# Counting edges per node and relation in a graph network: superblocks of layer 0 with every four groups in place of six, and a group's counts added two groups later

## The reference

```python
def _rgcn_layer(x, src, dst, edge_type, w_rel, root, bias):
    seg = dst * NUM_REL + edge_type                 # NUM_REL = 10
    sums = segment_sum(x[src], seg, N * NUM_REL)
    cnt = segment_sum(ones(seg.shape), seg, N * NUM_REL)
    mean = (sums / maximum(cnt, 1.0)[:, None]).reshape(N, NUM_REL, -1)
    return einsum('nrd,rdo->no', mean, w_rel) + x @ root + bias
edge_type = argmax(msg[:, 16:26], axis=1)
h = relu(_layernorm(x))
h = relu(_rgcn_layer(h, src, dst, edge_type, w_rel1, root1, b1))
x = x + _rgcn_layer(h, src, dst, edge_type, w_rel2, root2, b2)
```

## The kernel before

| u | TensorE | ScalarE |
| --- | --- | --- |
| 0 | | square root |
| 1 | transposes | norm and relu |
| 2 | root, chunks 0 to 3 | copy of the transposes |
| 3 | chunks 4 to 7 | copy of root, copies 0 to 3 |
| 4 | chunks 8 to 11 | copies 4 to 7 |
| 5 | | copies 8 to 11 |

## Time and profile before

### The profile page before, as it was taken

How to read it: one execution, slowest core, us unless ns; L and a number is a source line. 1 busy time by engine, 2 the same in 40 slices (tenths; PEclk the granted TensorE clock), 3 DMA queues, 4 the chain that set the end, 5 groups by cost and what they waited for, 6 DMA issues and landing times.

```text
span 17665.0 us, 179568 instructions
## 1 busy us (share of the span) xinstructions
PE 7873.9 (45%) x36107; PEld 6273.0 (36%) x36108; DVE 6843.6 (39%) x28057; ACT 3221.2 (18%) x6961; POOL 10730.4 (61%) x10236
## 2 busy tenths in 40 slices
PE   5633333623333333333333333333333577777777
PEld 3333333322222223332332322222222455555555
DVE  8522222244444423323322222344544344444443
ACT  3422222300000000000000000000000144444443
POOL 0266666365555546666566666666666268888882
PEclk8755555856666555555555555555555577777775
DMA  2333333411111131111111111233333266666665
GB/s 102 125 88 89 89 88 88 175 47 53 54 54 53 53 104 53 52 52 51 51 46 46 47 47 47 60 87 85 87 86 87 66 113 118 117 117 118 117 118 122
DMA packets 1122539, 1438.17 MB, mean 81 GB/s; under 512 B 211981, under 2 KB 737444, under 8 KB 1122316
## 3 DMA queue, kind: packets, MB, share of 16 engines
q0 software_dynamic: 536912, 792.85, 21.0%
q1 hardware_dynamic: 531700, 613.30, 11.9%
q10 hardware_dynamic: 53748, 30.36, 0.6%
HBM read 1101.27 MB, written 334.40 MB: 81 GB/s over the span
## 4 chain that ended last, share of the span: by engine, by line
another core or an unknown queue 29%; issue 22%; DVE 21%; DMA 10%; POOL 6%; PE 5%; ACT 3%; DVEq 2%; ACTq 1%; SPq 0%; POOLq 0%
DMA agg_dram<-acc,sum_row 9%; DVE tab_s L1950 5%; POOL agg_dram L887 5%; DVE scratch L1950 4%; DVE xn_h L1958 3%; DVE scratch L1920 3%; DVE acc L1906 2%; DVE rows L1818 1%; PE ps L1604 1%; POOL scratch L901 1%; ACT hT_s L1009 1%; PE ps L1361 1%; PE ps L1561 1%; PE ps L1562 1%
## 5 line engine op out<-in xcount | busy, mean ns | idle before, releaser
L901 POOL DMA_INDIRECT scratch<-table_dram,row_st x4160 | 3966.4, 953 | 2541.5 <-ACT row_st L1040 1269.3
L901 POOL DMA_INDIRECT rows<-table_dram,row_st x4160 | 3964.0, 953 | 2321.5 <-issue 1247.3
L1361 PE MATMUL ps<-tab_s,rows 128*128 128x128 f32 x8320 | 1906.8, 390 | 3028.0 <-issue 1274.0
L1361 PE MATMUL ps<-scratch 128*128 128x128 f32 x8320 | 1829.5, 390 | 2873.1 <-DMA scratch<-table_dram,row_st 1247.8
L887 POOL DMA_INDIRECT agg_dram<-acc,sum_row x1664 | 2654.5, 1595 | 529.2 <-issue 391.2
L1361 PEld LDWEIGHTS ps<-tab_s,rows 128*128 128x128 f32 x8320 | 1694.4, 294 | 3214.8 <-issue 2149.0
L1361 PEld LDWEIGHTS ps<-scratch 128*128 128x128 f32 x8320 | 1617.8, 289 | 3058.3 <-issue 2119.2
L1906 DVE TENSOR_TENSOR acc<-ps,acc 128x128 f32 x2080 | 608.6, 293 | 4575.8 <-remote 4054.7
L1950 DVE TENSOR_SCALAR scratch<-ps,rw_st 128x128 f32<-128x128 f32 x3328 | 1114.3, 401 | 338.4 <-issue 227.4
L1920 DVE SCALAR_TENSOR_TENSOR scratch<-iota,rw_st,ps 128x128 f32<-128x128 f32 x2496 | 715.2, 343 | 1355.3 <-remote 873.9
L1950 DVE TENSOR_SCALAR tab_s<-ps,rw_st 128x128 f32<-128x128 f32 x3328 | 1112.2, 401 | 330.3 <-issue 247.0
(11 more groups left out here) (229 smaller groups left out, 10600.9 us busy)
## 6 DMA issues: line engine op xcount, KB each, us to landing
scratch<-in_src_row SPq DMA_DIRECT2D x832, 256.0 KB
table_dram<-tab_s POOLq DMA_DIRECT2D x200, 640.0 KB, 3.2
scratch<-type_dram SPq DMA_DIRECT2D x416, 256.0 KB
scratch<-in_dst_row SPq DMA_DIRECT2D x416, 256.0 KB
rows<-table_dram,row_st POOLq DMA_INDIRECT x4160
scratch<-table_dram,row_st POOLq DMA_INDIRECT x4160
scratch<-table_dram SPq DMA_DIRECT2D x416, 64.0 KB
agg_dram<-acc,sum_row POOLq DMA_INDIRECT x1664
```

Of the source, the lines that this page charges most:

```text
L901: pool.indirect_dma_start(row_banks[bank][:, u, :], None, table_dram[k], bass.IndirectOffsetOnAxis(ap=row_st[:, bank, u:u + 1], axis=0)).t ...
L1361: mm = pe.matmul(ps[bank][:, q * P:(q + 1) * P], rows[:, u, :], hot[:, u, :], start=u % QUAD == 0, stop=u % QUAD == QUAD - 1)
```

## The change

`SPAN` goes from 6 to 4, so all 25 superblocks are woven into the first 100 groups, `left` is 0, and `early_rest` and `early_whole` do nothing. `STAGES`, the number of buffers for staged destinations, goes from 3 to 4. Root, chunks and copies are put into `u` 2 and 3: six chunks each, on both engines. The additions of group g-2 now stand inside VectorE's part of group g, one behind each four one-hots; the wait for the products of group g-2 stands ahead of the group. `flow_keep` and `flow_init` each get a wait for their own instruction.

```diff
-SPAN = 6
-STAGES = 3
+SPAN = 4
+STAGES = 4
...
                 elif u == 2:
                     early_hT(f)
+                    early_root(f, at)
+                    early_chunks(f, range(e_chunks // 2))
                 else:
-                    if u == 3:
-                        early_root(f, at)
-                    early_chunks(f, range((u - 3) * e_chunks // 3, (u - 2) * e_chunks // 3))
+                    early_chunks(f, range(e_chunks // 2, e_chunks))
...
                 if u == 2:
                     early_root(f)
-                if 2 <= u < 5:
-                    early_products(f, range((u - 2) * e_chunks // 3, (u - 1) * e_chunks // 3))
+                    early_products(f, range(e_chunks // 2))
+                if u == 3:
+                    early_products(f, range(e_chunks // 2, e_chunks))
...
                 dve.tensor_scalar(acc_f, acc_f, keep, bias_once, ALU.mult, ALU.add).then_inc(s_keep, 1)
+                dve.wait_ge(s_keep, so_far(reps, k, has_src, t) + 2)
...
+                dve.wait_ge(s_init, so_far(reps, k, has_root, t) + 2)
...
-            def count_group(r, g, u):
+            def count_group(r, g, u, before=None):

                 turn = dve.snap(r * ngroups + g)
                 bank = u % 2
+                if before is not None:
+                    t, win = dve.snap(turn - 2), windows(dve, before)
+                    dve.wait_ge(n_mm, t + 2)
                 dve.wait_ge(n_staged, turn + 1)
...
                     i.then_inc(n_hot, 1)
+                    if before is not None:
+                        window = counts[:, bass.ds(win[q], P)]
+                        dve.wait_ge(n_add, t * 4 + (q + 8))
+                        dve.tensor_tensor(window, ps[7 * bank][0:NCNT, q * P:(q + 1) * P], window, ALU.add).then_inc(n_add, 1)
...
                         for u in range(1, SPAN):
-                            count_group(r, u, u)
-                            count_adds(dve.snap(t0 + (u - 1)), u - 1, (u - 1) % 2)
+                            count_group(r, u, u, u - 2 if u > 1 else None)
```

More of the change, by code:

```diff
@@ L1864, in count_pass @@
                                 for u in range(SPAN):
-                                    count_group(r, dve.snap(first + u), u)
-                                    count_adds(dve.snap(t0 + first + (u - 1)), dve.snap(first + (u - 1)), (u + 1) % 2)
+                                    count_group(r, dve.snap(first + u), u, dve.snap(first + u - 2))
                                     if u == 0:
@@ L1870, in count_pass @@
                         g = SPAN * mixed + u
[L1871 to L1874, removed]
+                        count_group(r, g, u, g - 2 if g > 1 else None)
+                    for g in range(max(ngroups - 2, 0), ngroups):
+                        count_adds(dve.snap(t0 + g), g, g % 2)
                     dve.wait_ge(n_add, r * (4 * ngroups) + (4 * ngroups + 8))
```

## The result

| us | before | after |
| --- | --- | --- |
| median (14 runs of each, taken in turn) | 17678.61 | 17724.08 |
| lowest and highest | 17663.2, 17702.44 | 17695.3, 17800.06 |
| span of the profiled execution | 17665.0 | 17722.3 |
| counts stored (counting's end) | 627.57 | 758.51 |
| ScalarE begins the first pass | 772.77 | 806.86 |

The ratio is 1.0025, with a 95% interval of 1.0016 to 1.0034: the changed kernel is slower, by 45 us, where 54 were forecast. In the profiled executions the counting stage ends 130.9 later, the first pass over the edges begins 34.1 later, and the whole is 57 longer.

What follows compares the result with a forecast made beforehand. VectorE was taken to bound the counting before, a 25.7 us ring through three engines after. Counting ending at 776.6 instead of 627.57, plus a tail of 50 instead of 145, gave +54: median 17734 us, range 17672 to 17792.

Steps and rivals of the forecast that it cites:

- the ring: Counting: VectorE, TensorE and ScalarE wait for each other in a circle, 25.7 us per four groups, ends 24.0 to 28.1.
- rival C: Counting: VectorE keeps the beat, 19.1 us per superblock, the whole 105 us faster; chance 0.12.
- D: VectorE's time for one group with spread additions: 4.0 us, between 3.6 (additions at 0.19) and 4.37 (no gain).
- The last copy: ScalarE's last copy of a superblock ends 1.0 us behind TensorE's last chunk; ends 0.65 and 1.27.
- The reciprocal's step: VectorE, from the reciprocal to the next group, once per superblock: 0.48 us.
- The clock's 0.6: TensorE's clock falls while idle, slowing products and root: 0.6 us taken, between 0 and 1.96.
- The tail: From the counting's last addition to the first pass: 50 us instead of 145, being inverses computed, then loaded, then relation types.
- the chain: Behind the counting, computing the inverses until their loads are requested: 35.1 us, one norm fewer than 37.7.
- A: The forecast itself, ring from 24.9 us up: slower by 35 to 112 us; chance 0.61.
- B: Ring of 22.0 to 24.9 us, tail's gain and longer counting cancel: within 35 us; chance 0.22.
- The break-even ring: Ring length at which the longer counting just cancels the shorter tail: 23.45 us.
- The flow waits: Later passes, waits in `flow_keep` (75 times) and `flow_init` (50): 0 taken, at worst 0.22 each, 27 us.

Runs made afterwards that it cites:

- e3: Changed kernel with the next superblock's square root ahead of ScalarE's last three copies and the table loads out of the loop; ratio 0.9944 to before.
- e4: Changed kernel with the square root's activation table loaded once ahead of the counting, no order changed; ratio 0.9983 to before.
- e6: e3 with the additions of a group again behind all one-hots of the next group, table loaded once ahead of the loop; ratio 0.9952 to before.
- e1: Changed kernel with the four additions of a group again behind all one-hots of the next group; ratio 1.0010 to before.
- after_again: Changed kernel, unchanged, measured and profiled again on another chip; ratio 1.0019 to before.
- e5: Kernel before with only the two waits in `flow_keep` and `flow_init` added; 15558.66 us against 15558.56.
- e2: Changed kernel with `SPAN` 6, `STAGES` 3 and chunks placed as before, keeping the spread additions and flow waits; ratio 0.9977 to before.

## Why the prediction was right, point by point

- **What bounds it.** Right. That a ring takes over from VectorE when the second half of the copies stands ahead of the square root is what the timeline of after shows, and e3 and e4 turn it round: taking 2.56 off ScalarE's part of the ring won 2.60 per ring. The mechanism of rival C, VectorE keeping the beat, fell for this kernel, since its waits for the square root are 144.9 us; e6 is the kernel in which it holds.
- **The size of the ring.** 24.91 for 25.7, inside the ends given. **D** was 3.83 for 4.0: three of the four additions step by 0.20 (403.63 to 403.83), near the lower end of 0.19, where 0.29 was taken; the fourth, ahead of the next group's first instruction, still takes 0.39 (406.17 to 406.56 in the trace). The last copy ended 0.59 behind the chunks and not 1.0. The reciprocal's step went the other way, 1.07 for 0.48; e1, in which the load of the windows stands behind the group again, has 0.50. The working had named that load, but put it into D, where it is hidden, and not behind the reciprocal, where it is not. The clock's 0.6 stood between two cases that both occur, 3.08 - 2.03 = 1.05 and -0.08; the 1.96 of the upper end occurred in neither.
- **The counting's end.** 758.5 for 776.6. 24 rings of 0.8 too much are 19, and the start and the last superblock together were right within 1 us.
- **The tail.** 48.4 for 50: the chain 32.6 for 35.1, the landing of the inverses 12.5 for 11, the types 3.2 for 4. So 96.8 us were won there, and the counting gave back 130.9.
- **The sum.** +34.1 at the first pass where +54 was worked out; the total came to +45. The first comparison's 11 beyond the 34 are inside its interval (28 to 60), and after_again has +31. The later passes move by a few microseconds each way in the profiled executions (pass 1 +9.7, passes 2 to 4 -3.4, pass 5 +12.8), and no cause is shown for it. The forecast of the total was thus nearer than its working deserves: that it missed by 9 and not by 20 is luck. By the first pass's start, +34.1, and by the +31 of after_again, the result lies at the border of A (35 to 112) and B (within 35), not in the middle of A.
- **The break-even ring** of 23.45 is borne out: 24.91 gave +34.1 and e1's 24.07 gave +14.2, which by 24 rings puts it at 23.5 both times.
- **The rules weighed.** That chained operations take the same with and without a semaphore between is what the Trainium skill says (VectorE: DVE Perf Modes, "The DRAIN you can't avoid"); that other instructions between them win nothing either, so that D stays 4.37, was the prediction's own step from it. Here the group takes 3.83, and the additions' waits went from 41.4 to 0.0. That each table load brings 1.38 us of drain (the Trainium skill's ScalarE: Activation LUTs, "What ACT_TABLE_LOAD costs") is not what this case shows either: taking two out won 2.60, their durations alone.
- **The flow waits and `STAGES`.** The waits at nothing: right, by e5. Their worst price was misread: by the prediction's own 0.38 and 0.19 it is 0.19 each, 24 us and not 27. `STAGES` was not tried alone: the buffer is picked by `u % STAGES`, so `SPAN` has to be a multiple of it, and 3 does not go with `SPAN` 4 nor 4 with 6. In after VectorE waits for staging once, for 1.4 us.

What the prediction did not work out is that the change's two large edits work against each other. It named the burst of products, but gave no price to each edit alone. By the first pass's start, `SPAN` 4 alone costs 14, the additions alone win 31, and together they cost 34: with the additions behind a group, TensorE may take the next group's products alongside its one-hots (2.54 us from 394.07 in e1); with the additions among them it has to wait for that group's end (406.58, 410.40), and with `SPAN` 4 TensorE is on the ring.

## What to carry to other kernels

When work that ran behind a stage is woven into it, look for the circle that it closes among the engines, add up its terms once round, and compare it with the busiest engine's own time; the larger of the two is the beat. An edit that saves an engine work but lengthens the way round the ring costs time, as the spread additions did here. The cheapest cure is often order: a short operation that another engine waits for goes ahead of the long ones in its queue (it was worth 44 of the 106 us that e3 won in the counting, the table loads the rest). Of the kernels tried e3 and e6 are the fastest, by 0.56% and 0.48% against before; e2 and e4 are faster than before too, by 0.23% and 0.17%.

## What the runs showed of the hardware

- In after, VectorE shows no idle time between two groups (406.56), though the load of the windows (line 428) stands there, but about 0.7 us ahead of the first group behind a norm or a reciprocal: 49 times, 33.7 us in all. In e1, where that load and the wait for the products stand behind the one-hots, the step behind the reciprocal is 0.50 and not 1.07. That the load and not the wait makes the difference is argued, not shown.
- After an idle stretch of 7.8 us TensorE's granted clock was back at 1.00 before root in one ring and rose only within it in the next, and rings of equal work took 24.50 and 25.63 us.
- A table load on ScalarE costs its own 1.28 us and nothing besides: the next instruction begins 0.02 behind it (425.76 + 1.28 to 427.06), and without two loads the ring is 2.60 shorter (e4).
- The same kernel took 17679, 17859 and 15559 us on three chips, while its counting stage ended at 627.57 and 627.44 on the two of them that have a profile of it. A comparison of totals from different chips would show nothing here.
